# The expert passes of the last MoE layer: order of matmuls, source of the second weights, scatters and final sums

## The reference, cut to what matters

```python
# _L1_ffn_ref: h = layernorm(x), 1024 tokens, 16 experts, hidden width 176, top 6
logits = h @ gate_w.T
scores = softmax(logits); topk_w, topk_idx = top_k(scores, 6)
cw = zeros((T, 16)).at[arange(T)[:, None], topk_idx].add(topk_w)
for e in range(16):
    g = h @ w_gate[e].T
    u = h @ w_up[e].T
    out = silu(g) * u @ w_down[e].T
    y = y + cw[:, e:e + 1] * out
x = x + y
```

## Time and profile before

| | us |
|---|---|
| timed runs (median; lowest to highest of 3) | 876.45; 874.01 to 876.85 |
| profiled execution | 867.91 |
| its span in the profile | 866.1 |
| PE busy in it | 789.5 (91%) |
| DVE, ACT, POOL busy | 507.1, 400.1, 278.8 |
| PE's share of the chain that ended last | 62% |

### The profile page before, as it was taken

One profiled execution on the slowest core, in us unless ns is written; L12 is line 12 of the kernel. 1 busy time (PEld: TensorE's weight loads), 2 busy tenths in 40 slices (PEclk: granted clock), 3 DMA queues, 4 the chain that ended last, 5 costly groups with the idle time before them and its releaser, 6 DMA issues.

```text
span 866.1 us, 15945 instructions
## 1 busy us (share of the span) xinstructions
PE 789.5 (91%) x5107; PEld 521.6 (60%) x5107; DVE 507.1 (59%) x1270; ACT 400.1 (46%) x856; POOL 278.8 (32%) x374
## 2 busy tenths in 40 slices
PE   5988799889979998999999999899899999999990
PEld 3566566676557785777777767667654444444440
DVE  5999876666512236756556655777534763443564
ACT  3987777555123333443233342232527454555540
POOL 3643744113500033111111111137602265554430
PEclk9998999999989999999999999999979999999995
DMA  4002770181253221044453533113232243537316
GB/s 140 2 1 37 244 257 2 35 238 51 80 165 109 86 67 56 19 142 134 134 159 122 171 92 78 53 50 101 90 68 68 62 126 116 135 117 245 101 46 212
DMA packets 103590, 91.22 MB, mean 105 GB/s; under 512 B 38104, under 2 KB 95448, under 8 KB 103512
## 3 DMA queue, kind: packets, MB, share of 16 engines
q1 hardware_dynamic: 93288, 67.92, 27.2%
q0 software_dynamic: 6912, 19.28, 6.4%
q10 hardware_dynamic: 3312, 3.02, 1.0%
HBM read 50.47 MB, written 38.67 MB: 103 GB/s over the span
## 4 chain that ended last, share of the span: by engine, by line
PE 62%; DVE 12%; issue 6%; POOL 5%; DMA 4%; ACT 3%; DVEq 0%; ACTq 0%; SPq 0%; POOLq 0%
PE bank L1383 8%; PE bank L1346 7%; PE bank L673 7%; PE bank L1240 6%; PE bank L1226 5%; PE bank L699 5%; PE bank L896 3%; PE bank L2166 3%; POOL rows L771 3%; PE bank L918 2%; PE bank L657 2%; PE bank L2123 2%; PE bank L2150 2%; DMA rows<-arena,sidx 2%; PE bank L685 2%
## 5 line engine op out<-in xcount | busy, mean ns | idle before, releaser
L1487 ACT ACTIVATE arena<-bank 128x512 f32<-128x512 f32 (+1 forms) x96 | 46.9, 525 | 147.5 <-PE bank L1346 147.4
L1138 POOL TENSOR_TENSOR arena<-arena,causal_t 128x256 f32<-128x256 f32 x64 | 45.1, 726 | 214.0 <-ACT arena L1492 214.0
L781 POOL DMA_INDIRECT ret<-arena,ridx x64 | 66.1, 1033 | 103.9 <-ACT arena L747 49.9
L673 PE MATMUL bank<-arena 128*64 (+1 forms) x512 | 91.0, 477 | 1.0 <-DVE arena L733 1.0
L1383 PEld LDWEIGHTS bank<-arena 128*128 128x128 f32 x640 | 76.6, 192 | 5.2 <-POOL arena L1138 2.7
L1383 PE MATMUL bank<-arena 128*128 128x129 f32 x640 | 77.5, 276 | 1.7 <-POOL arena L1138 1.7
L1346 PE MATMUL bank<-arena 128*128 128x512 f32 (+3 forms) x256 | 75.7, 440 | 1.4 <-DVE arena L1546 1.4
L699 PE MATMUL bank<-arena 88*64 (+1 forms) x512 | 69.8, 393 | 3.2 <-DVE arena L725 1.7
L754 DVE TENSOR_TENSOR arena<-arena,bank 128x176 f32<-128x176 f32 x64 | 21.6, 337 | 86.2 <-ACT arena L741 86.0
L1240 PE MATMUL bank<-arena 128*128 128x256 f32 x256 | 62.6, 389 | 1.5 <-DVE arena L1553 1.5
L1240 PEld LDWEIGHTS bank<-arena 128*128 128x128 f32 x256 | 49.4, 194 | 22.6 <-issue 12.1
(11 more groups left out here) (288 smaller groups left out, 1527.0 us busy)
## 6 DMA issues: line engine op xcount, KB each, us to landing
rows<-arena SPq DMA_DIRECT2D x16, 544.0 KB, 4.6
rows_in<-place SPq DMA_DIRECT2D x5, 1664.0 KB, 14.4
arena<-rows SPq DMA_DIRECT2D x64, 128.0 KB, 2.1
arena<-in_w_gu SPq DMA_DIRECT2D x24, 256.0 KB, 3.5
arena<-ret SPq DMA_DIRECT2D x12, 512.0 KB, 6.7
arena<-in_w_dn SPq DMA_DIRECT2D x24, 176.0 KB
arena<-in_wq SPq DMA_DIRECT2D x32, 128.0 KB, 3.9
arena<-in_wo SPq DMA_DIRECT2D x32, 128.0 KB, 2.0
```

What stands on the lines that cost most here:

```text
L673: mm = nc.tensor.matmul(p_gu[J % 2][u * HR:(u + 1) * HR, 0:2 * FE].rearrange("p (y n) -> p y n", y=2), pxT[:, J % 2, k, u * HR:(u + 1) * H ...
L781: nc.gpsimd.indirect_dma_start(ret[h], bass.IndirectOffsetOnAxis(ap=ridx[:, h, j:j + 1], axis=0), py[J % NY], None).then_inc(s_ret, 16)
L1138: nc.gpsimd.tensor_tensor(blocks, blocks, causal_t[:].unsqueeze(1).to_broadcast([P, 2, P]), ALU.mult).then_inc(s_p, 1)
L1487: nc.scalar.activation(th[:, sbank * 512:sbank * 512 + w], b_s[sbank][:, 0:w], ACT.Tanh, scale=SCALE / SOFTCAP).then_inc(s_th, 1)
```

## The change

The passes are written in another order on PE, DVE and ACT. On PE, pass J of the loop has turn(J+2), hidden(J-1), gate-up(J+1), down(J-1), where it had turn(J+2), gate-up(J+1), hidden(J), down(J-1). The pieces of layer norm and routing are moved by about one pass. `pair_y` is DVE's now, `pair_copy_dn` is gone: SP loads the second expert's down weights for each pass from DRAM (`load_dn_pair`). The first half's scatters go in groups of 5, the second half's 24 without a wait between them. `rows1_back(0)` stands ahead of `pair_x(0)`. Of the last sums DVE does two of four tiles of each table; PE does the others as products with diagonal matrices of router weights (`spread_weights`, `sum_back`), and DVE adds their sum.

```diff
-            for y, w in enumerate((GU1, 2 * DIM)):
-                nc.vector.tensor_scalar(tab1[:, h, y, :], c.ej, float(E1 - 1), float(w), ALU.min, ALU.mult).then_inc(s_tab, 1)
+            nc.vector.tensor_scalar(tab1[:, h, 0, :], c.ej, float(E1 - 1), float(GU1), ALU.min, ALU.mult).then_inc(s_tab, 1)
+            for u, w in enumerate((2 * DIM, FE)):
...
-            pe.wait_ge(s_wbd, J + 1)
+            pe.wait_ge(s_wbd[J % 2], wbd_0[J % 2] + 16 * (J // 2 + 1))
...
-            nc.vector.tensor_copy(wbd[0:HB, J % 2, :], w1_dn[0:HB, bass.ds(off, 2 * DIM)]).then_inc(s_wbd, 1)
...
-            nc.scalar.copy(py[J % NY], p_y).then_inc(s_pye, 1)
+            nc.vector.tensor_copy(py[J % NY], p_y).then_inc(s_pye, 1)
...
-                else:
-                    pool.wait_ge(s_rows, SC + SC1 * h + 64 * g)
...
+            elif h == 0:
+                pool.wait_ge(s_rows, SC + 16 * lo)
...
+        def spread_weights(self, dve, k):
...
+        def sum_back(self, pe):
+            pe.wait_ge(s_rx1, 3)
+            for k in range(K1):
+                pe.wait_ge(s_ys[k], ys_0[k] + 32)
+                for t in (2, 3):
+                    mm = nc.tensor.matmul(b_y[0][:, (t - 2) * DIM:(t - 1) * DIM], dg[:, 2 * k + t - 2, :], ys[k][:, t, :],
+                                          start=(k == 0 and t == 2), stop=(k == K1 - 1), skip_group_check=True)
+            mm.then_inc(s_y, 1)
...
+        def load_dn_pair(self, sp, J):
+            off = self.owner(sp, J, 1, 1)
+            if J >= 2:
+                sp.wait_ge(s_pyd, NB + J - 1)
+            back = io["w_dn1"].rearrange("i p d -> (i p) d")
+            sp.dma_start(wbd[0:HB, J % 2, :].rearrange("p (q d) -> p q d", q=2),
+                         back[bass.ds(off, FE), :].rearrange("(q p) d -> p q d", p=HB)).then_inc(s_wbd[J % 2], 16)
...
-            for J in range(2 * NP1):
-                self.load_rows(sp, J)
-                if J % NP1 == 1:
+            for J in range(2 * NP1 + 4):
+                if J < 2 * NP1:
+                    self.load_rows(sp, J)
+                if J >= 4:
+                    self.load_dn_pair(sp, J - 4)
+                if J in (1, NP1 + 1):
...
-                if 25 <= n < 31:
-                    self.send_rows(pool, 0, (n - 25,))
+                if 25 <= n < 30:
+                    self.send_rows(pool, 0, 5 * (n - 25), min(5 * (n - 24), 4 * K1))
...
+                    self.rows1_back(dve, 0)
                     self.pair_x(dve, 0)
                     self.pair_x(dve, 1)
                     self.pair_mul(dve, 0)
...
             for J in range(2 * NP1):
+                if J:
+                    self.pair_h(dve, J - 1)
...
+                if J:
+                    self.pair_y(dve, J - 1)
...
+            self.pair_h(dve, 2 * NP1 - 1)
+            self.pair_y(dve, 2 * NP1 - 1)
             for i in range(4 * K1):
-                self.add_back(dve, 1, i)
+                if i % 4 < 2:
+                    self.add_back(dve, 1, i)
+            dve.wait_ge(s_y, NH + 1)
+            self.residual(dve, 6, b_y[0])
```

More of the change, by code:

```diff
@@ L705, in owner @@
             if q == u:
-                eng.wait_ge(s_tab, 3 + 2 * (h + 1))
-            return eng.value_load(tab1[0:1, h, y, q:q + 1], min_val=0, max_val=(E1 - 1) * (GU1, 2 * DIM)[y])
+                eng.wait_ge(s_tab, 3 + 3 * (h + 1))
+            step = (GU1, (2 * DIM, FE)[u])[y]
+            return eng.value_load(tab1[0:1, h, y, q:q + 1], min_val=0, max_val=(E1 - 1) * step)
         def pair_copy_gu(self, act, J):
@@ L760, in pair_h, with send_rows @@
             nc.vector.tensor_copy(phT[0:HB, J % 2, :, :], p_h[0:HB, :].rearrange("p (q n) -> p q n", q=2)).then_inc(s_pte, 1)
[L762 to L767, removed]
-                else:
-                    pool.wait_ge(s_rows, SC + SC1 * h + 64 * g)
-                for i in range(4 * g, 4 * g + 4):
-                    nc.gpsimd.indirect_dma_start(rows1[h], bass.IndirectOffsetOnAxis(ap=sidx1[:, h, i % K1, i // K1:i // K1 + 1], axis=0),
-                                                 xa[h][:, i // K1, :], None).then_inc(s_rows, 16)
+        def send_rows(self, pool, h, lo, hi):
+            if lo == 0:
+                pool.wait_ge(s_pl, DI1[h])
+                pool.wait_ge(ln_xn, NT + 20 + 4 * h)
+                pool.wait_ge(s_zf, ZF1)
+            elif h == 0:
+                pool.wait_ge(s_rows, SC + 16 * lo)
+            for i in range(lo, hi):
+                nc.gpsimd.indirect_dma_start(rows1[h], bass.IndirectOffsetOnAxis(ap=sidx1[:, h, i % K1, i // K1:i // K1 + 1], axis=0),
+                                             xa[h][:, i // K1, :], None).then_inc(s_rows, 16)
         def send_back(self, pool, J):
@@ L1139, in pool @@
                                             ALU.mult).then_inc(s_p, 1)
-                if 25 <= n < 31:
-                    self.send_rows(pool, 0, (n - 25,))
+                if 25 <= n < 30:
+                    self.send_rows(pool, 0, 5 * (n - 25), min(5 * (n - 24), 4 * K1))
             for J in range(2 * NP1):
                 if J == R0:
-                    self.send_rows(pool, 1, range(K1))
+                    for t in range(4):
+                        self.send_rows(pool, 1, t * K1, (t + 1) * K1)
                 self.send_back(pool, J)
@@ L1389, in pe @@
                     self.pair_turn(pe, J + 2)
+                if J:
+                    self.pair_hidden(pe, J - 1)
+                if J == 4:
+                    pe.wait_ge(s_xres.sem, 12)
+                    self.ln_turn(pe, 10)
+                    self.ln_turn(pe, 11)
+                if J == 1:
+                    self.turn(pe, NH - 1)
+                if J == 5:
+                    self.logits(pe, 3)
+                if J == 11:
+                    self.places1(pe, 1)
+                if J == 2:
+                    self.project(pe, NH - 1)
                 if J + 1 < 2 * NP1:
@@ L1393, in pe @@
                     offs.append(owners(J + 3))
-                self.pair_hidden(pe, J)
                 if J:
                     self.pair_down(pe, J - 1, offs[J - 1])
[L1397 to L1408, removed]
+            self.pair_hidden(pe, 2 * NP1 - 1)
             self.pair_down(pe, 2 * NP1 - 1, offs[2 * NP1 - 1])
+            self.sum_back(pe)
         def silu(self, act, M):
@@ L1679, in dve @@
             for J in range(2 * NP1):
+                if J:
+                    self.pair_h(dve, J - 1)
+                if J == 1:
+                    self.turned(dve, NH - 1)
                 if J + 1 < 2 * NP1:
                     self.pair_mul(dve, J + 1)
[L1682 to L1687, removed]
                 if J == 2:
@@ L1710, in dve @@
                     self.rows1_weights(dve, 1)
-                if J == 14:
+                if J == 15:
                     self.rows1_edges(dve, 1)
-                if J == 15:
+                if J == 16:
                     self.rows1_table(dve, 1)
-                if J == 16:
+                if J == 17:
                     self.rows1_owner(dve, 1)
+                if NP1 + 8 <= J < NP1 + 8 + K1:
+                    self.spread_weights(dve, J - NP1 - 8)
                 if J == NP1 + 2:
```

53 lines of the change are left out of this document (28 added, 25 removed).

## The result

The changed kernel takes 915.37 us (median of 4; 913.52 to 923.49) beside 875.23 (median of 4; 873.90 to 876.85): ratio 1.0476, 95% interval 1.0409 to 1.0542. The direction was forecast, the size (884.1, at most 893) was not. The profiled execution took 915.9 us, span 914.1, PE busy 795.5.

What follows compares the result with a forecast made beforehand. PE was taken as the bound, busy 95.0 of 100 us in the pass stage. Terms -12.4 + 15.4 + 2.5 + 5.5 - 6.8 - 1.5 + 5 = +7.7 on the median 876.45 gave 884.1 us, range 861 to 893.

Steps and rivals of the forecast that it cites:

- width changes: PE's steady passes: two changes between narrow and wide matmuls instead of four, 0.2 us a pass over 62 passes, -12.4 us.
- late hidden rows: Down products of the early passes: PE waits for DVE's hidden-row copy behind routing blocks, 20.4 us instead of 5.0, +15.4.
- clock: Behind new long waits of PE: the granted clock falls, each may cost 1.7 us; +5 taken, bounds 0 and 9.
- queue ahead of down(47): Down weights of pass 47 by DMA stand behind six 512 KB loads of returned rows: +5.5 us, bounds 0 and 9.
- passes 62 and 63: Loop's end: no gate-up between hidden and down, and h(63) behind y(62) and two adds, +2.5 us.
- start: Stage's start: the 3.26 us row wait and half-clock loss go, 1.4 us of waiting comes; -6.8 us, bounds -2 and -8.
- end: Last sums: about 2 us instead of 3.5 after the last arrival, -1.5 us, bounds -2 and +1.
- Rival (c): PE's passes: width changes don't get cheaper, as gaps come from weights that can't be loaded ahead; 896.5 us, chance 0.04.
- Rival (a): Early passes: hidden rows are in time all the same; 862.1 us, or 856.6 if the queue holds nothing up; chance 0.22.
- rival (b): Waits for hidden rows come, but neither clock nor queue adds to them; 873.6 us, chance 0.16.
- So whether the scatters drain between them decides nothing: Second half's 24 scatters: with some 15 us of room up to pass 28, leaving out the drains costs nothing.
- Rival (d): 24 undrained scatters stall POOL, and the returns, beyond the 15 us of room; 889.1 us at 20 us more, chance 0.05.

Runs made afterwards that it cites:

- e9: The changed kernel without any edit, run again on a third chip: 889.57 us, 1.0276 of the kernel before.
- e1: The changed kernel with the second half's 24 scatters again in six groups of four, each waiting for the one before: 901.26 us, 1.0332 of the kernel before.
- e2: The kernel before without the waits between the second half's six groups of four scatters: 894.58 us, 1.0236 of the kernel before.
- e11: The kernel before without any edit, run again on the third chip for its trace: 866.64 us.
- e12: e7 with two PSUM banks for the hidden rows and the last sums on two engines: 853.44 us, 0.9863 of the kernel before.
- e6: The kernel before with the new order of PE's pass alone, weights still copied and scatters in fours: 876.93 us, 1.0097 of the kernel before.
- e7: e6 with down(J-2) in place of down(J-1) behind gate-up(J+1): 859.95 us, 0.9924 of the kernel before.
- e15: The changed kernel with the first half's returned rows loaded one table every second pass instead of six at once: 883.32 us, 1.0209 of the kernel before.
- e5: e1 with the down weights copied by DVE again, on another chip: 886.76 us, 1.0231 of the kernel before.
- e16: The changed kernel with e15's loads, down(J-2) for down(J-1), two PSUM banks for hidden rows and second-half scatters in fours: 864.95 us, 0.9987 of the kernel before.
- e10: e2 unchanged, run again on the third chip: 864.49 us, 0.9957 of the kernel before.
- e13: e2's kernel (the kernel before, second-half scatters undrained) a third time, on a fourth chip: 865.44 us, 0.9985 of the kernel before.
- e17: The kernel before without any edit, on a fifth chip, for its trace: 877.54 us.

## Why the prediction was right or wrong

First the two sorts of chips. Three chips without late signals give for the kernel before 866.8 to 868.2 us, two with them 873.5 and 874.2; the result's 875.23 and its trace of the changed kernel (213 of 368 records) belong to the second sort, the trace of before that the prediction read (368 of 368) to the first. By these numbers the gap of 8.5 us between that trace and the median was this effect, and it was added to the sum unexplained. On the result's chip the change costs 40.1 us, of which e9 shows 21.4 without late signals. The other 19 are late signals. Draining the scatters again (e1) gives back 14.1 of them; the remaining 5 or so are, by subtraction, what bursts of four cost the changed kernel more than the kernel before, which has them too. In the kernel before the same run of 24 cost 21 (e2).

What e9 and e11 give for each term, by the starts of gate-up (spans 887.6 and 864.8, +22.8):

| term | predicted | measured | how |
|---|---|---|---|
| width changes | -12.4 | -16.5 | busy time of PE, 1 to 20: 59.26 (e12) - 63.77; then 43 passes x 0.28 |
| late hidden rows, passes 1 to 20 | +15.4 | +10.6 | idle 14.0 - 3.4 |
| clock, passes 1 to 20 | part of +5 | +15.4 | busy 74.69 - 59.26 |
| queue ahead of down(47), with its clock | +5.5 | +12.0 | passes 36 to 52: 56.55 - 49.07 + 16 x 0.28 |
| passes 20 to 36 and 52 to 63 beyond their width | 0 | +1.2 | 46.00 - 49.73 and 30.65 - 33.26, + 27 x 0.28 |
| passes 62 and 63 | +2.5 | +2.4 | gate-up(63) to the last down matmul: 8.40 - 6.00 |
| start | -6.8 | -1.35 | gate-up(1) at 637.79 - 639.14 |
| end | -1.5 | -0.9 | from there to the span's end: 19.55 - 20.43 |

**Width changes: right, and larger.** 2.79 a pass, not 2.87: 0.28 for two changes less, where the earlier trace rows gave 0.2. Rival (c) is out.

**Hidden rows late: right.** e6 alone shows it: 15.0 us of waits for L760 in 7 places, against the sum's 20.4 in 11, so part of the blocks was covered and the term of +15.4 was too large by 4.8 (e9: +10.6). e7 and e12 confirm the mechanism by taking it away. Rival (a) is out.

**Clock: the mis-sized step on every chip, +5 in the sum and +15.4 in the first 20 passes alone.** I took half of 3.4 us for each long wait. Across the first 20 passes PE's busy time rises with its idle time instead: 3.7 idle and 59.3 busy at 1.00 (e12), 8.3 and 62.6 at 0.95 (e7), 16.4 and 69.6 at 0.86 (e6), 14.0 and 74.7 at 0.81 (e9). These are mean clocks between the two levels, 1.2 and 2.4 GHz; the waits every few passes kept the clock at the lower one for a large part of what lay between, so rival (b) was wrong too. It is no proportion: e15, whose first 20 passes are those of the changed kernel, has 16.5 idle and 71.6 busy at 0.85, the same sum as e9 within 0.6 us. The weights by DMA are not the cause: e5, which copies the weights, has 21.5 idle and 73.1 busy at 0.84, and e16, which loads them, 9.0 and 62.4 at 0.93, close to e7.

**Weights by DMA: mechanism right, size short.** The wait for the load was 8.1 where +5.5 stood (bounds 0 and 9), and the clock fell behind it (0.91 over passes 36 to 52, has the six loads). e15 takes away 10.7 of the 12.0. The rule that I cited from the Trainium skill (DMA: Bandwidth & Descriptors, Queues, rings and completion order), that a ring's descriptors are consumed in ring order, agrees with this trace. A gain was missed: taking DVE's copies away is worth 5.9 us in the first 20 passes (94.6 in e5, 88.7 in e9, on two chips).

**Start: wrong.** The sum had PE wait 1.4 us behind pair_x(0). It waited 0.89 for that copy and then 3.88 ("issue") ahead of gate-up(0), where before had 1.04. The wait has no releaser because PE's own sequencer was at work: between turn(1) and gate-up(0) it reads six weight addresses, one every 0.65 us. The kernel before does the same, but there it reads most of them while the matmuls of the projection (L1240) still run, from 628.29 to 631.91. In the changed kernel the projection had ended at 626.31, before `pair_x(0)` let turn(1) start, and the reads had nothing beside them. The sum left them out. They are, in the changed kernel and in the kernel before:

```profile
L713 PEldq TENSOR_LOAD <-tab x6: 301/307/318, 627.2 to 630.5; - x6
```

```profile
L707 PEldq TENSOR_LOAD <-tab x6: 300/305/308, 629.1 to 632.4; - x6
```

And the clock fell all the same. From the timeline of PE in the changed kernel:

```profile
627.20 0.41 PE L662 MATMUL bank<-ident,arena 128*128 128x128 f32 x2 [0.89 <-DVE arena L730]
631.49 2.61 PE L678 MATMUL bank<-arena 128*64 x8 [3.88 <-issue]
```

Gate-up(0), 1.40 in a steady pass, takes 2.61. The gain of 1.35 us lies even past the bound of -2 ("if the clock falls all the same").

**End and passes 62, 63: right** within 0.6 us each.

**"So whether the scatters drain between them decides nothing": the step that failed by most.** On a chip without late signals it stands (e10, e13). On the sort of the result's chip the drain decides 14.1 us in the changed kernel (e1) and 21 in the kernel before (e2), where the sum had 0. Rival (d) named the edit but priced POOL's room, 15 us; POOL went on at 1.27 us a scatter, it was PE's signals that stopped. Nothing in the profile of before pointed to it except the unexplained 8.5 us. That and the clock, with the queue and the start behind them, are why 884.1 became 915.4. The Trainium skill (SBUF — State Buffer, Who interferes with whom) has it that DMA never contends with a compute engine for SBUF's ports; these runs do not contradict that, since the products end in time by the profile's (modelled) ends and only their signals come late, but the stops lie beside POOL's transfers, and grow when these are not drained.

Open: what in a chip makes PE's signals late, why PE's alone, and why those traces miss records of semaphores; the two always came together, and nothing here tells which causes which, or whether recording has a part in it. Each chip was seen in one series of runs alone, so it isn't shown either that a chip keeps its sort. Whether a pause between scatters does as well as a drain wasn't tried.

## What to carry to other kernels

Before a chain of copies is moved next to its consumer, count what its engine does in between: the regrouping was worth 16 us, waits that came with it took more than that, and one pass more of distance plus a second buffer (e7, e12) turned +1% into -1.4%, small gains at the end included. Price waits of TensorE with the clock: here 10.6 us of new idle time came with another 15.4 of slower matmuls. When a wait goes, look at what the engine's own sequencer did in its shade: six address reads came out as 3.9 us. Keep runs of indirect transfers short even where their own engine never stalls, and when a trace and the timed median differ by 1%, find out why before a sum is made on either.

## What the runs showed of the hardware

While POOL issues indirect transfers back to back, TensorE's semaphore increments can arrive up to 27.2 us after its products end by the profile; those of ACT and DVE, where recorded, don't. It happened on two of five chips, and in the result: up to 22.3 us for 24 in a run (e2), 0.5 to 4.5 us in bursts of four (e1, e17). The same kernel takes 866.6 us on one chip (e11) and 877.5 on another (e17); 7.6 us of that lie in passes 20 to 36, beside the scatters.

An address read by PE's sequencer (TENSOR_LOAD and what goes with it) takes 0.65 us, hidden beside running matmuls and in the open without them.
